# Decoder layer on one core: score banks read in pairs, folded weights in four parts, half of the variances on ScalarE, a new order

## What is computed

```python
# 1. FFT attention, with a residual and a norm
qf, kvf = l2norm(fft(x @ W_q.T, per head)), l2norm(fft(x @ W_kv.T, per head))
values = ifft(qf * cumsum(kvf, axis=tokens)).real
x1 = layernorm(x + values @ W_o.T)
# 2. causal softmax attention against a given context (keys = values = ctx)
scores = x1_heads @ ctx_heads.T / 4, masked where key > query
x2 = layernorm(x1 + softmax(scores) @ ctx_heads)
# 3. a feed-forward step on ternary inputs
xq = 0.5 where x2 > 0.33, -0.5 where x2 < -0.33, else 0
out = layernorm(x2 + xq @ (ternary(weight, 0.2, 0.6) + rram_variation).T)
```

## Time and profile before

| | |
|---|---|
| median of 3 runs | 153.93 us (152.79 to 154.58) |
| the profiled execution, whole | 154.16 us |
| its span, first to last instruction | 152.4 us |
| outside the span | 1.76 us |
| granted TensorE clock, mean | 0.993 |
| DMA traffic | 19.33 MB, mean 127 GB/s |

### The profile page before, as it was taken

The page is one execution under the profiler, slowest core; times in us unless marked ns, Lnnn a source line. Parts: engine busy times, 40 slices in busy tenths (PEclk is TensorE's granted clock), DMA queues, the critical chain, the costliest instruction groups (busy, mean ns, idle before and its releaser), DMA issues.

```text
span 152.4 us, 4763 instructions
## 1 busy us (share of the span) xinstructions
PE 135.7 (89%) x1737; PEld 91.5 (60%) x1737; DVE 131.9 (87%) x420; ACT 115.5 (76%) x318; POOL 100.5 (66%) x212
## 2 busy tenths in 40 slices
PE   6999999999999799999999989999897988996540
PEld 2944657455674447766575856776675867674330
DVE  0036999999989699998999989999998999999972
ACT  3126655777694687979998999989999799978940
POOL 4020252536856457757989789799999889998542
PEclk9999999999999999999999999999999999999997
DMA  3897962231159404453283226845469951202212
GB/s 101 269 245 263 308 227 42 102 77 63 39 148 237 138 0 137 123 158 75 36 224 105 52 52 137 282 127 176 106 201 125 178 144 22 69 4 69 75 69 71
DMA packets 25208, 19.33 MB, mean 127 GB/s; under 512 B 13152, under 2 KB 21088, under 8 KB 25184
## 3 DMA queue, kind: packets, MB, share of 16 engines
q1 hardware_dynamic: 25184, 19.02, 47.5%
HBM read 14.16 MB, written 2.10 MB: 107 GB/s over the span
## 4 chain that ended last, share of the span: by engine, by line
PE 42%; DVE 22%; POOL 9%; SPq 7%; ACT 6%; issue 6%; DMA 5%; POOLq 0%
PE p L823 11%; DVE x L2101 8%; PE p L877 5%; PE p L843 5%; PE p L870 4%; POOL probs L418 4%; DMA x1T_b<-x_b 3%; PE p L897 3%; SPq L198 3%; POOL rstd L412 3%; PE p L829 3%; PE p L794 2%; ACT probs L1462 2%; PE p L799 2%; PE p L853 2%
## 5 line engine op out<-in xcount | busy, mean ns | idle before, releaser
L418 POOL TENSOR_SCALAR_AFFINE_SELECT probs<-probs 128x512 f32<-128x512 f32 x64 | 41.2, 663 | 8.6 <-ACT probs L1462 7.9
L2101 DVE TENSOR_REDUCE x<-p 128x4 f32<-128x512 f32 x64 | 41.7, 679 | 2.3 <-PE p L853 2.3
L1462 ACT ACTIVATE probs<-p 128x512 f32<-128x512 f32 x64 | 34.9, 602 | 4.3 <-PE p L870 4.2
L823 PE MATMUL p<-w_in,xT_s 128*128 128x512 f32 x64 | 30.2, 601 | 0.0
L412 POOL TENSOR_TENSOR rstd<-ve,power 128x1 f32<-128x1 f32 x48 | 27.6, 577 | 2.8
L1480 ACT ACTIVATE dev<-r,neg 128x256 f32<-128x256 f32 x41 | 21.0, 515 | 2.4 <-DVE neg L2074 2.4
L877 PE MATMUL p<-probs,vals 128*32 128x128 f32 x512 | 19.5, 278 | 0.7 <-ACT probs L1462 0.3
L870 PE MATMUL p<-x1T,keys 32*128 32x128 f32 x512 | 18.8, 283 | 1.0 <-ACT yT_s L1450 0.4
L870 PEld LDWEIGHTS p<-x1T,keys 32*128 32x128 f32 x512 | 15.7, 186 | 5.7 <-DVE x L2101 2.1
L407 POOL TENSOR_SCALAR ve<-spread 128x1 f32<-128x1 f32 x48 | 10.2, 212 | 13.1 <-ACT dev L1480 10.0
L823 PEld LDWEIGHTS p<-w_in,xT_s 128*128 128x128 f32 x64 | 11.4, 190 | 10.2 <-issue 9.1
(11 more groups left out here) (81 smaller groups left out, 252.2 us busy)
## 6 DMA issues: line engine op xcount, KB each, us to landing
keys<-ctxK SPq DMA_DIRECT2D x16, 256.0 KB, 3.6
vals<-ctxV SPq DMA_DIRECT2D x16, 256.0 KB, 3.2
xT_s<-xT SPq DMA_DIRECT2D x16, 128.0 KB, 3.0
x_s<-x SPq DMA_DIRECT2D x16, 128.0 KB, 3.2
out<-res SPq DMA_DIRECT2D x16, 128.0 KB, 2.3
wq_s<-w_q SPq DMA_DIRECT2D x1, 256.0 KB, 2.7
wkv_s<-w_kv SPq DMA_DIRECT2D x1, 256.0 KB, 3.8
fv_s<-ffn_vT SPq DMA_DIRECT2D x1, 256.0 KB, 3.4
```

What stands on the lines that cost most here:

```text
L418: nc.gpsimd.affine_select(out=part, in_=part, compare_op=ALU.is_ge, fill=0.0, base=0, pattern=[[0, GH], [1, TOK]], channel_multiplier=-1). ...
L823: last = nc.tensor.matmul(p[PROJ[n]][:], xT_s[n % XR][:, g, :], w_in[:, g, :], start=(g == HALVES[0]), stop=(g == HALVES[1]))
L1462: nc.scalar.activation(probs[n % 2][:, c, :, :].rearrange("p g q -> p (g q)"), p[SCORES[n][c]][:], ACT.Exp, scale=HD ** -0.5).then_inc(exp ...
L2101: nc.vector.tensor_reduce(x1[n % X1R][:, c::GH, HD], p[APPROX[n][c]][:].rearrange("p (h k) -> p h k", h=GH), AX.X, ALU.max, negate=True).t ...
```

## The change

1. **Pairs of banks.** The eight PSUM banks become one tensor, and `row_max`, `exponentials` and `mask` take two banks or two parts at once: 32 instructions of 1024 elements per partition in the place of 64 of 512, for each of the three. The bank tables give neighbouring banks to each pair. The semaphores are per pair, so what waits for a part now waits for its pair.
2. **Folded weights in four parts.** The first key/value half and the DFT matrix come in one DMA (192 KB), the second key/value half and the first query half (128 KB each) are issued from ACT's queue, the second query half from SP's. The key/value products are made first, each part has its own bank, and is copied by an instruction of its own (256 columns; ACT two, DVE two). `project(0)` is made in two column halves, key/value first. 5 + 1 warming matmuls in the place of 7 + 2.
3. **Variances.** 23 of the 48 `variance` steps run on ACT as an activation over a 128x1 tile (`spread` x 1/256 + eps); 25 stay on POOL. The roots stay on POOL.
4. **Other moves.** Three of DVE's four `normalise_x1` go to ACT (15 and 1 now). ACT has 16 `copy_outT` (15 before, and one on DVE), 9 `result` (10; DVE 7, 6 before), 5 `copy_xqT` (6; one now on DVE), 15 `round_x1` (16; one now on DVE). Two `ternary_above` go from DVE to POOL. Two more `shift_of` on DVE. For element 0, the bf16 `x1` is transposed by PE and copied by ACT, no longer by DMA.
5. **New order.** All five lists, and the bank tables, are written anew.

The arithmetic on every element is the same.

```diff
-        p = [bank(f"p{i}", [128, CW]) for i in range(8)]
+        banks = bank("banks", [128, 8, CW])
+        p = [banks[:, b, :] for b in range(8)]
+        def two_banks(b):
+            return banks[:, b[0]:b[1] + 1:b[1] - b[0], :]
...
             def mask(n, c):
                 pool.sem_inc(mask_go, 1)
-                part = probs[n % 2][:, c, :, :]
+                part = probs[n % RING][:, 2 * c:2 * c + 2, :, :].rearrange("p c g q -> p (c g) q")
                 nc.gpsimd.affine_select(out=part, in_=part, compare_op=ALU.is_ge, fill=0.0, base=0,
-                                        pattern=[[0, GH], [1, TOK]], channel_multiplier=-1).then_inc(masked[c], 1)
+                                        pattern=[[0, 2 * GROUPS], [1, TOK]], channel_multiplier=-1).then_inc(masked[c], 1)
...
             def exponentials(n, c):
-                nc.scalar.activation(probs[n % 2][:, c, :, :].rearrange("p g q -> p (g q)"), p[SCORES[n][c]][:], ACT.Exp,
-                                     scale=HD ** -0.5).then_inc(exps[c], 1)
+                nc.scalar.activation(probs[n % RING][:, 2 * c:2 * c + 2, :, :].rearrange("p c g q -> p c (g q)"),
+                                     two_banks(SCORES[n][2 * c:2 * c + 2]), ACT.Exp, scale=HD ** -0.5).then_inc(exps[c], 1)
...
             def row_max(n, c):
-                nc.vector.tensor_reduce(x1[n % X1R][:, c::GH, HD],
-                                        p[APPROX[n][c]][:].rearrange("p (h k) -> p h k", h=GH), AX.X, ALU.max,
-                                        negate=True).then_inc(maxed[c], 1)
+                nc.vector.tensor_reduce(x1[n % X1R][:, :, HD].rearrange("p (g s) -> p s g", s=GH)[:, 2 * c:2 * c + 2, :],
+                                        two_banks(APPROX[n][2 * c:2 * c + 2]).rearrange("p b (h k) -> p b h k", h=GH), AX.X, ALU.max,
+                                        negate=True).then_inc(maxed[c], 1)
...
+            def variance(n, i):
+                nc.scalar.activation(ve[i][n % RING][:], spread[i][n % RING][:], ACT.Identity, bias=eps[:], scale=1.0 / DIM).then_inc(ve_done_act[i], 1)
...
+            def project_half(n, k, ready):
+                cols = slice(k * DIM, (k + 1) * DIM)
+                for g in range(2):
+                    pe.wait_ge(ready[g], 1)
+                    last = nc.tensor.matmul(p[PROJ[n]][:, cols], xT_s[n % XR][:, g, :], w_in[:, g, cols],
+                                            start=(g == 0), stop=(g == 1))
+                return last
...
+            act.dma_start(wkv1_s[:], kv_1).then_inc(in_kv, 16)
+            act.dma_start(wq_s[0][:], w_q[0]).then_inc(in_q[0], 16)
             act.preload_act_table_set("natural_log_exp_and_others")
```

More of the change, by code:

```diff
@@ new lines, in _ @@
+            root(6, 0)
+            pool.wait_ge(ve_done_act[1], 2)
+            root(2, 1)
+            pool.wait_ge(x2_done, 3)
+            ternary_above(2)
+            pool.wait_ge(ve_done_act[0], 6)
+            root(7, 0)
+            pool.wait_ge(exps[0], 5)
+            mask(4, 0)
+            pool.wait_ge(exps[1], 5)
+            mask(4, 1)
+            pool.wait_ge(straight, 10)
+            y_real(9)
+            pool.wait_ge(var[2], 2)
+            variance(1, 2)
+            pool.wait_ge(ve_done[2], 1)
@@ L643, in _ @@
+            variance(13, 0)
             root(6, 1)
-            mask(8, 0)
+            pool.wait_ge(x2_done, 7)
+            ternary_above(6)
+            y_imaginary(15)
+            root(13, 0)
             pool.wait_ge(exps[0], 10)
@@ L1188, in _ @@
+            transpose_x1(7)
+            attend(11)
+            pe.wait_ge(maxed[0], 9)
+            pe.wait_ge(x1T_copied, 8)
+            score(7)
+            pe.wait_ge(maxed[1], 9)
+            pe.wait_ge(masked[0], 7)
             pe.wait_ge(vals_in[0], 32)
             weigh(6, 0)
-            pe.wait_ge(maxed[3], 9)
+            weigh(6, 1)
+            pe.wait_ge(masked[1], 7)
+            weigh(6, 2)
+            weigh(6, 3)
+            pe.wait_ge(added[0], 12)
+            transpose_y(12)
@@ L1583, in _ @@
+            round_x1(2)
+            deviations(3, 0)
+            act.wait_ge(var[0], 4)
+            variance(3, 0)
+            act.wait_ge(pv_done[2], 1)
+            copy_outT(0)
+            act.wait_ge(x1T_done, 2)
+            copy_x1T(1)
+            act.wait_ge(scored, 2)
+            exponentials(1, 0)
+            exponentials(1, 1)
+            copy_yT(5)
+            act.wait_ge(neg_done[1], 1)
+            deviations(0, 1)
             act.wait_ge(ssq_done, 9)
             log_norms(8)
-            exponentials(0, 3)
@@ L1652, in _ @@
-            deviations(1, 1)
-            log_norms(11)
+            act.wait_ge(var[0], 7)
+            variance(6, 0)
+            act.wait_ge(var[2], 1)
+            variance(0, 2)
+            act.wait_ge(pv_done[3], 4)
+            copy_outT(3)
+            act.wait_ge(x1_done_act, 5)
+            round_x1(5)
+            variance(2, 1)
+            act.wait_ge(shift_done[2], 1)
+            result(0)
+            act.wait_ge(ssq_done, 12)
+            log_norms(11)
+            act.wait_ge(x1T_done, 5)
@@ L1654, in _ @@
+            copy_x1T(4)
+            act.wait_ge(lnA_done, 12)
+            root_norms(11)
+            act.wait_ge(neg_done[0], 8)
+            deviations(7, 0)
+            normalise_x1(6)
             act.wait_ge(proj, 13)
             square(12)
-            act.wait_ge(lnA_done, 12)
-            root_norms(11)
+            act.wait_ge(rsA_done, 12)
+            square_roots(11)
+            act.wait_ge(var[0], 8)
+            variance(7, 0)
+            act.wait_ge(scored, 5)
+            exponentials(4, 0)
@@ L1719, in _ @@
+            act.wait_ge(neg_done[0], 10)
+            deviations(9, 0)
+            act.wait_ge(var[2], 3)
+            variance(2, 2)
+            act.wait_ge(scored, 6)
+            exponentials(5, 0)
+            act.wait_ge(shift_done[2], 3)
+            act.wait_ge(stored[0], 16)
+            result(2)
+            exponentials(5, 1)
+            normalise_x1(8)
             act.wait_ge(proj, 15)
             square(14)
-            act.wait_ge(scored, 6)
-            exponentials(5, 1)
-            exponentials(5, 2)
@@ L1754, in _ @@
+            round_x1(9)
+            act.wait_ge(x1T_done, 8)
+            copy_x1T(7)
+            act.wait_ge(neg_done[1], 6)
+            deviations(5, 1)
+            normalise_x1(10)
+            act.wait_ge(neg_done[2], 4)
+            deviations(3, 2)
+            act.wait_ge(scored, 8)
+            exponentials(7, 0)
+            exponentials(7, 1)
+            act.wait_ge(yT, 13)
+            copy_yT(12)
             act.wait_ge(ssq_done, 16)
             log_norms(15)
+            copy_outT(6)
@@ L1965, in _ @@
             deviations(15, 2)
+            act.wait_ge(var[2], 16)
+            variance(15, 2)
         @block.vector
```

2866 lines of the change are left out of this document (1342 added, 1524 removed).

## The result

The changed kernel takes 155.95 us (median; 155.63 to 156.19), the kernel before in the same comparison 153.78. The ratio is 1.0143, with a 95% interval of 1.008 to 1.0206. The prediction said 151.3, with faster by over 1% as the likely case; it was wrong. The profiled execution took 156.19 us, 1.8 of it outside the span.

What follows compares the result with a forecast made beforehand. DVE, busy 95.5% from 24 to 140 us, was taken to bound the kernel. -2.6 - 1.2 + 1.9 + 0.5 - 1.5 = -2.9 gave a span of 149.5, so 151.3 us with the time outside it; range 148.7 to 154.6.

Steps and rivals of the forecast that it cites:

- Pairs on DVE, -2.6: Row maxima on DVE read two banks at once, saving the fixed part of 32 instructions: -2.6 us.
- Moved steps, -1.2: Steps moved off and onto DVE, such as three normalise_x1 to ACT, change its work by -1.2 us together.
- the start, -1.5: First square 0.3 us earlier, and two weight steps moved into DVE's early idle time (-1.2): together -1.5 us.
- Pair waits, +0.5: Whoever waits for one part now waits for two: +0.5 us on DVE's idle time in the middle.
- ACT +4.2 and POOL -9.3: Changes in engine work from pairs, variances and moved steps: ACT +4.2 us, POOL -9.3 us.
- Rivals 1 and 2: Late stretch is POOL's: 149.3 us, chance 0.20; ACT, 93.5% busy from 80 to 133, takes over: 153.6, chance 0.13.
- I take +1.9: DVE's short steps, stretched beside POOL's masks, wait longer beside pair masks: +1.9 us on today's 4.3.
- The third rival: A pair mask on POOL locks out DVE's shifts and x2 scalings: +6.7 us for the holds, 156.1 us, chance 0.15.
- The argument against the rival: Medians of DVE's stretched steps are 60 ns above the minima, so most instances aren't met by a mask.
- The rival's own test: The mean of DVE's shift should be 0.25 to 0.3 us; at 0.5 the mask lock-out would hold.
- not below 131: Sign against the forecast: DVE's busy time, expected near 130.0 us, not falling below 131.

Runs made afterwards that it cites:

- singles: The changed kernel with all three pairs undone (64 instructions of 512 each for maxima, exponentials and masks): 153.80 us, ratio 1.0005 against the kernel before.
- split2: The changed kernel with each pair mask made by two instructions of 512 elements: 153.78 us, ratio 0.9971 against the kernel before.
- var_pool_split2: The changed kernel with masks of 512 elements and all 48 variances on POOL: 156.06 us, ratio 1.0158 against the kernel before.
- tiny: The changed kernel with each pair mask cut to 8 of its 1024 elements: 150.01 us, ratio 0.9669 against the kernel before.
- before_shift_ts: The kernel before with only the shift rewritten as a tensor_scalar with rstd as scalar operand: ratio 1.0000 against the kernel before.

## Why the prediction was wrong

Step by step, as the sum had them:

- **Pairs on DVE, -2.6: held as a duration.** The maxima went from 41.7 to 38.2 us. It bought little: undone, the time moves by 0.1 to 0.3%.
- **Moved steps, -1.2, and the start, -1.5: not contradicted.** The start's gain shows at the first row maximum (1.7 us earlier here; in singles 1.9, in split2, with the same start, 1.0). The moved steps weren't tried alone.
- **Pair waits, +0.5: no sign of it.** DVE's idle time between 24 and 140 fell by 1.0.
- **ACT +4.2 and POOL -9.3: +3.9 and -8.2.** A variance costs ACT 288 ns, within its bounds. Rivals 1 and 2 are answered: POOL's relief is worth something (var_pool_split2), but the late stretch isn't POOL's alone, as its 17.0 of 20 us after 120 shows; ACT doesn't take over.
- **"I take +1.9" for the longer holds: the step that failed.** The mechanism was in the sum, its size was a third of what came: DVE's busy time is 6.8 us above what the other terms leave, and the loss over four lines grew by 6.0.
- **A term that the sum didn't have: the clock, +1.3.** With 6.0 for the holds, nothing for the pair waits and the rest as forecast, -2.6 - 1.2 + 6.0 - 1.5 = +0.7; with the clock's 1.3 that is +2.0, as the spans show (154.4 and 152.4). The third rival had +6.7 for the holds and 156.1 as the time; the profiled execution took 156.19. Its mechanism is right, its time agrees so well by luck, since it had neither the clock nor the missing pair waits.

Why +1.9 was too small can be read in the numbers. I took today's loss and scaled it with the mask's length (1.6) and its share of POOL's time (41%), that is, as often hit as before and longer. The factor for the length holds in the new order, 8.6 against the 5.3 of singles; in the old it is 2.2 (5.8 against 2.6). Three things are wrong in the rest. The share was too low: almost without masks, in tiny, 1.1 of the 8.6 us are left. Then, the loss counted only shifts and scalings. In the changed kernel `xq` and the addition lose 4.3 of the 8.6 us, before 0.8. Last, the new order changed how often the two meet, which the sum put at nothing. singles has the old mask length and the new order (with the moved steps), and a loss of 5.3, against 2.6 before: the order gives +2.7, and the length +3.3 to the changed kernel's 8.6. Counted by instances over 60 ns above the median, 11 steps are held before, 17 in singles and 18 in the changed kernel. A count in the lists points the same way without naming the steps: of the roots that a DVE shift waits for, a mask follows at once on POOL behind 9 of 24 now (6 of these shifts are held, but not the longest, 1033), and behind 5 of 22 before (1 is held, and 4 others are). The argument against the rival, that medians lie near the minima, was true (and still is, 156 beside 144) and beside the point: a few instances held for up to 0.9 us make the sum.

The rival's own test was badly set too. It said that it holds at a shift's mean of 0.5; the mean is 0.309, and the rival holds, since 4.9 of the 8.6 us lie on other lines. The tests by DVE's sum ("not below 131") were the ones that told.

The Trainium skill (SBUF — State Buffer, Who interferes with whom) names what is held off: DVE instructions with two SBUF inputs, against a GpSimd instruction that reads SBUF, for its whole length, and DVE's copies and `tensor_scalar` where they run in a two-port mode. The trace agrees: `neg` with one input takes 154 ns at most, the one-input shift 212 at most, and the two-input one 1033; of the 256-wide `tensor_scalar` steps the longest `x<-r,neg,rstd` took 907. The prediction cited this section, and gave the rival built on it 0.15. The earlier trace rows had shown the same thing in this kernel, and it should have been the base of the sum.

**Still open:** why the 1.5 us of the start and the relief of ACT don't show more at the end of singles (1.0005). Its DVE is busy 132.9 us against 131.9, so the order's own added loss of 2.7 us would cover it, but that isn't shown: no kernel here has the new order and the full masks without that loss. Open too is what makes the clock fall at 146 in one kernel, at 112 in another and behind the last matmul in a third.

## What to carry to other kernels

Merging instructions saves their fixed part on the engine that runs them, and makes every hold on a shared resource longer; on GpSimd, next to a VectorE that is the bound, weigh it by the instances that are held (mean minus median, times the count), not by the busy time saved. Before merging or moving a GpSimd step, list which two-input SBUF steps of VectorE can fall beside it. A product of per-partition numbers can be written with a scalar operand there: some 50 ns dearer, and in 118 instances of five profiles never over 216 ns. That pays where the holds are many (the new order) and gave nothing where they are few (before_shift_ts). Splitting has its limit as well: at 256 elements the fixed part made GpSimd the one that is waited for. And before a difference of 1% is explained, compare the granted clock of the last stretch on both sides.
